# Two self-attentions of a decoder: scores with the keys as the stationary side, and a softmax over two halves of the keys

## What is computed

```python
# layer 0 (layer 1: same sizes, bias = -slope_h * sqrt(i - j) under the causal mask)
q = (x @ wq.T).reshape(B, N, 32, 128).transpose(0, 2, 1, 3)
k = (x @ wk.T).reshape(B, N, 8, 128).transpose(0, 2, 1, 3)      # 8 groups of 4 heads
v = (x @ wv.T).reshape(B, N, 8, 128).transpose(0, 2, 1, 3)
s = einsum('bhgnd,bhmd->bhgnm', q, k) * scale                    # 64 x 64 per batch and head
p = softmax(where(causal, s, -inf))
o = einsum('bhgnm,bhmd->bhgnd', p, v)
x = layernorm(x + o @ wo.T)
```

## Time and profile before

| | |
|---|---|
| median of 3 runs | 2332.91 us (2332.28 to 2333.55) |
| the profiled execution | 2332.89 us, its span 2331.0 us |
| PE busy | 2224.3 us, 95% of the span |
| DVE / ACT / POOL busy | 1300.0 / 781.4 / 772.1 us |
| first self-attention, second self-attention | about 0 to 563 us, about 1080 to 1680 us |
| DMA queue of SP | 22.4% of 16 engines' span |

### The profile page before, as it was taken

The page is one execution under the profiler, slowest core; times in us unless marked ns, Lnnn a source line. Parts: engine busy times, 40 slices in busy tenths (PEclk is TensorE's granted clock), DMA queues, the critical chain, the costliest instruction groups (busy, mean ns, idle before and its releaser), DMA issues.

```text
span 2331.0 us, 33907 instructions
## 1 busy us (share of the span) xinstructions
PE 2224.3 (95%) x11762; PEld 1769.8 (76%) x11762; DVE 1300.0 (56%) x2151; ACT 781.4 (34%) x1475; POOL 772.1 (33%) x709
## 2 busy tenths in 40 slices
PE   8999999997999989999899999999989999999978
PEld 6888888885555547887788888888878888887867
DVE  3454444447677733334345444444766767766766
ACT  2233222223677742222233232222333333232321
POOL 4222222202343336344422122221454344434233
PEclk9999999999999999999899999999999999999989
DMA  4212221221000032230222332222222222222120
GB/s 165 72 58 79 81 79 51 68 55 47 12 17 18 14 126 95 86 108 0 86 72 65 82 82 73 55 73 55 70 65 68 61 61 81 63 72 54 32 78 37
DMA packets 120545, 152.41 MB, mean 65 GB/s; under 512 B 16272, under 2 KB 67984, under 8 KB 119952
## 3 DMA queue, kind: packets, MB, share of 16 engines
q1 hardware_dynamic: 120464, 151.33, 22.4%
HBM read 124.02 MB, written 27.26 MB: 65 GB/s over the span
## 4 chain that ended last, share of the span: by engine, by line
PE 80%; issue 7%; DVE 7%; POOL 4%; ACT 2%; DMA 0%; POOLq 0%; DVEq 0%; ACTq 0%; SPq 0%
PE banks L283 20%; PE banks L285 19%; PE banks L284 18%; PE banks L598 7%; PE banks L641 3%; PE banks L1279 3%; PE banks L1263 2%; POOL f_wl L1690 1%; PE banks L1245 1%; PE banks L1252 1%; PE banks L1215 1%; PE banks L1231 1%; POOL f_il L1698 1%; DVE st L351 1%; PE banks L1269 1%
## 5 line engine op out<-in xcount | busy, mean ns | idle before, releaser
L283 PE MATMUL banks<-xTh,wh 128*128 128x512 f32 x1024 | 418.5, 409 | 11.7 <-DVE xTl L1965 7.5
L285 PE MATMUL banks<-xTh,wl 128*128 128x512 f32 x1024 | 404.3, 395 | 0.0
L284 PE MATMUL banks<-xTl,wh 128*128 128x512 f32 x1024 | 403.2, 394 | 0.0
L283 PE MATMUL banks<-woh,oth 128*128 128x512 f32 x768 | 313.5, 408 | 16.3 <-DVE X L936 7.0
L284 PE MATMUL banks<-wol,oth 128*128 128x512 f32 x768 | 301.8, 393 | 0.0
L285 PE MATMUL banks<-woh,otl 128*128 128x512 f32 x768 | 301.7, 393 | 0.0
L1031 POOL TENSOR_TENSOR sc_sb<-sc_sb,rs 128x512 f32<-128x512 f32 x96 | 103.7, 1083 | 553.2 <-DVE rs L890 553.2
L936 DVE TENSOR_TENSOR X<-banks,X 128x512 f32<-128x512 f32 x192 | 132.0, 688 | 272.9 <-PE banks L285 272.0
L733 ACT ACTIVATE q_sb<-banks 128x512 f32<-128x512 f32 x192 | 114.6, 597 | 402.0 <-PE banks L285 402.0
L283 PEld LDWEIGHTS banks<-xTh,wh 128*128 128x128 f32 x1024 | 195.2, 191 | 52.5 <-issue 9.3
L285 PEld LDWEIGHTS banks<-xTh,wl 128*128 128x128 f32 x1024 | 194.6, 190 | 43.6
(11 more groups left out here) (214 smaller groups left out, 4010.6 us busy)
## 6 DMA issues: line engine op xcount, KB each, us to landing
raw<-in_a_in SPq DMA_DIRECT2D x144, 256.0 KB, 2.8
raw<-in_a_out SPq DMA_DIRECT2D x96, 256.0 KB, 2.8
turned<-pq SPq DMA_DIRECT2D x384, 64.0 KB, 1.8
pt<-turned SPq DMA_DIRECT2D x96, 256.0 KB, 2.8
f_q<-in_f_q SPq DMA_DIRECT2D x21, 512.0 KB, 3.8
f_s<-in_f_s SPq DMA_DIRECT2D x21, 512.0 KB, 5.3
X<-in_x SPq DMA_DIRECT2D x1, 2048.0 KB, 10.7
x_craw<-in_ctx SPq DMA_DIRECT2D x8, 256.0 KB, 2.7
```

The lines of the kernel that those rows point to most:

```text
L283: nc.tensor.matmul(out, w_hi, x_hi, start=start, stop=False)
L284: nc.tensor.matmul(out, w_hi, x_lo, start=False, stop=False)
L285: return nc.tensor.matmul(out, w_lo, x_hi, start=False, stop=stop)
```

## The change

In `attn0` and `attn1`:

- The score product is turned: 64 columns of k are stationary and all 256 query columns move. Four calls a pair, 8 instructions; the calls with `b = 0` write partitions 0 to 63, those with `b = 1` partitions 64 to 127 of the same bank. A key now stands on each partition.
- DVE transposes 32x32 blocks straight from PSUM. A partition then holds a query and 32 of its 64 keys; the other 32 keys are 32 partitions away. DVE scales and adds the bias (now laid out for this, `bias_t`), and maximum, subtraction, exponential and sum go over each half apart.
- New event `SW`: PE multiplies the 32 columns of maxima and sums with a permutation matrix (`swap`), which brings each partition the numbers of the other half. New event `SX`: DVE copies them, subtracts the maxima, caps at 80; ACT takes the exponential; DVE multiplies, adds and takes the reciprocal. POOL normalises.
- A second DVE transposition of 32x32 blocks puts the keys back on the partitions, directly into `pt`. `turned` is no longer used there: 64 times five DMAs go. The bias of `attn1` comes in 8 DMAs a group, not 2.
- The list of events is new, and all engines follow it as it stands: `later` and `order` go. In the changed kernel the line numbers are higher.

The diff, cut to the parts that matter:

```diff
+        ev = events("U_0 VT1- SU3- PT0- SX2- U_1 SW3- TR2- SX3- WS0- WS1- U_2 PV0- PT1- TR3- WS2- WS3- U_3 WO0- PV1- U_4 PT2- "
+                    "WO1- U_5 PV2- WO2- SC0 SD0 EX0 PT3- WO3- SC1 SU0 SD1 EX1 U_6 PV3- SW0 WO4- SX0 SU1 U_7 SW1 TR0 WO5- SX1 "
+                    "U_8 TR1 WO6- U_9 WO7- SC2 SD2 EX2 U_10 SU2 SC3 SD3 EX3 U_11 SW2 VT0")
     if not project:
         if rms:
             return events("PT0- PV0- WO6-- SS3- PT1- WO7-- WS0- WS1- SC2- SD2- WS2- WS3- EX2- SU2- PV1- SC3- TR2- WO0- SD3- EX3- "
...
-            sq_turned = sb("sq_turned", [P, 32, 32])
+            sq_turned = shared[:, :].rearrange("p (n d) -> p n d", n=32)
+            bias_t = shared[:, 0:256]
...
-                        src = st.bias_in[i, r] if isinstance(i, int) else \
-                            st.bias_in[bass.ds(i, 1), r].rearrange("o p n -> p (o n)")
-                        sp.dma_start(bias[r, :, :], src.rearrange("p (c g s) -> p c g s", c=2, g=2)[:, :, h, :]
-                                     ).then_inc(ld_b, 16)
+                    for k in range(4):
+                        for h in range(2):
+                            r = slice(32 * h, 32 * h + 32)
+                            src = st.bias_in[i, r] if isinstance(i, int) else \
+                                st.bias_in[bass.ds(i, 1), r].rearrange("o p n -> p (o n)")
+                            sp.dma_start(bias_t[32 * k:32 * k + 32, :].rearrange("q (g h s) -> q g h s", g=G, h=2)[:, :, h, :],
+                                         src.rearrange("q (g s) -> q g s", g=G)[:, :, 32 * (k % 2):32 * (k % 2) + 32]
...
-                    if before and c in (1, 3) and not st.rms:
-                        move_out(i - 1, 2 + c // 2)
-                    if before and c in (2, 4) and not st.rms:
-                        move_in(i - 1, 1 + c // 2)
...
+                if not st.rms:
+                    for m in range(4):
+                        t, b = m // 2, m % 2
+                        col = pair * 2 * P + m * S
+                        last = nc.tensor.matmul(pb[2][64 * b:64 * b + 64, t * G * S:(t + 1) * G * S], k_sb[:, col:col + S],
+                                                q_sb[:, 4 * (pair % 2) + m, :], start=True, stop=True)
+                    last.then_inc(A["sc_done"], 1)
+                    return
                 for c in range(2):
                     for m in range(4):
                         col = pair * 2 * P + m * S
...
+            def swap_halves(i, pair):
+                st.need(pe, "s_sum", 4 * i + pair + 1)
+                st.need(pe, "s_link", 5 * (4 * i + pair) - 4)
+                if isinstance(i, int) and i == 0 and pair == 0:
+                    pe.wait_ge(A["swap_set"], 2)
+                nc.tensor.matmul(pb[4][:, 32 * pair:32 * pair + 32], swap[:, :], stat[:, pair, :], start=True,
+                                 stop=True).then_inc(A["s_swap"], 1)
 
             def square_sums(i, j):
...
                             r = slice(64 * b, 64 * b + 64)
-                            last = nc.tensor.matmul(PVB[b][:, cols], v_part[r, 2 * pair + t, :], by_query[p_part][r, t],
+                            p = by_query[p_part][r, t] if st.rms else (pth, ptl)[p_part][r, cols]
+                            last = nc.tensor.matmul(PVB[b][:, cols], v_part[r, 2 * pair + t, :], p,
                                                     start=v_part is vh and p_part == 0, stop=v_part is vl)
...
                         v_high(j, n)
-                    elif kind == ("EX" if st.rms else "SC"):
+                    elif kind == "EX":
                         exponentials(j, n)
+                    elif kind == "SX":
+                        st.need(act, "s_link", 5 * (4 * j + n) + 3)
+                        nc.scalar.activation(rel[:, n, :], rel[:, n, :], ACT.Exp).then_inc(A["s_rel"], 1)
                     elif kind == "PT":
-                        pt_wait(act, st, j, n, 1)
+                        if st.rms:
+                            pt_wait(act, st, j, n, 1)
+                        else:
+                            st.need(act, "t_done", 4 * j + n + 1)
...
-                        last = nc.vector.scalar_tensor_tensor(
-                            sc_sb[:, pair, 4 * c:4 * c + 4, :],
-                            pb[2][:, c * 4 * S:(c + 1) * 4 * S].rearrange("p (t s) -> p t s", t=4), st.scale, b[:, c],
-                            ALU.mult, ALU.add)
-                    last.then_inc(A["s_out"], 1)
+                    whole = rows.rearrange("p c s -> p (c s)")
+                    by_key = whole.rearrange("p (c k) -> p c k", k=32)
+                    nc.vector.transpose(whole, pb[2][:, :]).then_inc(A["s_turn"], 1)
+                    st.need(dve, "s_turn", 4 * i + pair + 1)
+                    if st.per_head_bias:
+                        two = whole.rearrange("p (t n) -> p t n", t=2)
+                        both = bias_t.rearrange("p (o n) -> p o n", o=1).to_broadcast([P, 2, G * S])
+                    else:
+                        two = rows
+                        both = bias_t[:, 0:S].rearrange("p (o n) -> p o n", o=1).to_broadcast([P, 8, S])
+                    nc.vector.scalar_tensor_tensor(two, two, st.scale, both, ALU.mult, ALU.add).then_inc(A["s_out"], 1)
                     st.need(dve, "s_out", 4 * i + pair + 1)
+                    nc.vector.tensor_reduce(stat[:, pair, 0:16], by_key, AX_X, ALU.max).then_inc(A["s_max"], 1)
+                    st.need(dve, "s_max", 4 * i + pair + 1)
+                    nc.vector.tensor_tensor(by_key, by_key, spread(stat[:, pair, 0:16]), ALU.subtract).then_inc(A["s_sub"], 1)
+                    return
                 nc.vector.tensor_reduce(smax[:, pair, :], rows, AX_X, ALU.max).then_inc(A["s_max"], 1)
                 st.need(dve, "s_max", 4 * i + pair + 1)
                 nc.vector.tensor_tensor(rows, rows, spread_rows(smax[:, pair, :]), ALU.subtract).then_inc(A["s_sub"], 1)
 
+            def spread(col):
+                return col.rearrange("p (c o) -> p c o", o=1).to_broadcast([P, 16, 32])
+
+            def relate_halves(i, pair):
+                link = 5 * (4 * i + pair)
+                st.need(dve, "s_swap", 4 * i + pair + 1)
+                nc.vector.tensor_copy(other[:, pair, :], pb[4][:, 32 * pair:32 * pair + 32]).then_inc(A["s_link"], 1)
+                st.need(dve, "s_link", link + 1)
+                nc.vector.tensor_tensor(rel[:, pair, :], other[:, pair, 0:16], stat[:, pair, 0:16],
+                                        ALU.subtract).then_inc(A["s_link"], 1)
+                st.need(dve, "s_link", link + 2)
+                nc.vector.tensor_scalar(rel[:, pair, :], rel[:, pair, :], 80.0, None, ALU.min).then_inc(A["s_link"], 1)
+                st.need(dve, "s_rel", 4 * i + pair + 1)
+                nc.vector.tensor_tensor(total[:, pair, :], other[:, pair, 16:32], rel[:, pair, :],
+                                        ALU.mult).then_inc(A["s_link"], 1)
+                st.need(dve, "s_link", link + 4)
+                nc.vector.tensor_tensor(total[:, pair, :], total[:, pair, :], stat[:, pair, 16:32],
+                                        ALU.add).then_inc(A["s_link"], 1)
+                st.need(dve, "s_link", link + 5)
+                nc.vector.reciprocal(inv[:, pair, :], total[:, pair, :]).then_inc(A["s_rec"], 1)
+
             def sums(i, pair):
                 st.need(dve, "exp_done", 4 * i + pair + 1)
+                if not st.rms:
+                    rows = sc_sb[:, pair, :, :].rearrange("p c s -> p (c s)").rearrange("p (c k) -> p c k", k=32)
...
 
                 st.need(dve, "p_ready", 4 * i + pair + 1)
+                if not st.rms:
+                    st.need(dve, "pt_ready", 4 * i + pair - 1)
+                    nc.vector.transpose(pt[:, pair % 2, :],
...
@@ -913,8 +992,10 @@
                         q_square_sums(j, n)
                     elif kind == "SS":
                         q_mean_square(j, n)
-                    elif kind == ("SD" if st.rms else "SC"):
...
             def normalise(i, pair):
                 st.need(pool, "s_rec", 4 * i + pair + 1)
                 rows = sc_sb[:, pair, :, :]
+                if not st.rms:
+                    rows = rows.rearrange("p c s -> p (c s)").rearrange("p (c k) -> p c k", k=32)
+                    nc.gpsimd.tensor_tensor(rows, rows, inv[:, pair, :].rearrange("p (c o) -> p c o", o=1).to_broadcast(
+                        [P, 16, 32]), ALU.mult).then_inc(A["p_ready"], 1)
+                    return
```

More of the change, by code:

```diff
@@ L439, in pt_wait @@
         def pt_wait(eng, st, i, pair, more):
-            wait(eng, pt_in[pair % 2], 16 * (16 * st.index + 2 * i + pair // 2 + more))
+            wait(eng, pt_in[pair % 2], 16 * (2 * i + pair // 2 + more))
         def late_bank(st, t):
@@ L518, in step @@
             def step(i, before, more):
-                first, second = (1, 2) if st.rms else (0, 1)
                 for c in range(5):
```

92 lines of the change are left out of this document (54 added, 38 removed).

## The result

The changed kernel takes 2380.05 us, median of 4 runs (2379.19 to 2383.95), the kernel before beside it 2333.23 (2332.28 to 2334.78). The ratio is 1.0203, 95% interval 1.0186 to 1.0221: 47 us slower, where +24 was forecast. The profiled execution of the changed kernel is the longest of its four, 2383.95 us with a span of 2382.0.

The account below looks back on a forecast made before the run. PE was taken to bound the kernel, busy 329.82 of 330 us. Its work -17, steady waits +32, first groups +3 and tails +6 made +24 us on 2332.91: 2357 us, range 2318 to 2388.

Parts of the forecast that it names:

- the term of the waits: PE's waits in steady groups of both self-attentions: 2.3 us in each of 7 groups of 2 stages, +32 us.
- the main case: Whole kernel: partial overlap in the score product plus new PE waits, 2357 us (2342 to 2370), chance 0.38.
- rival 2: Score product: no overlap between column halves, 2.0 us a product, +0.43 a pair, kernel 2389 us; chance 0.22.
- Scratch trips: Self-attentions: removing the trips gives 1.2 us at the most, counted as zero.
- Score product: PE, each pair: the turned product takes about 1.3 us instead of 1.79, -0.5, bounds +0.2 and -0.7.
- rival 3: Score product: column halves overlap fully, -0.47 a pair with the swap product, kernel 2347 us; chance 0.13.
- Swap product: PE, each pair: the added 128x32 product costs 0.23 us in full, 64 times.
- Swap of pair 1: PE in each steady group waits 1.2 us for DVE's sum of pair 1.
- First output tile: Steady groups: low parts 0.9 us late, last weight parts 0.4 more; not all new, so PE waits +0.8 us.
- The 0.3 at the swap of pair 3: Steady groups: PE waits 0.3 us there for the first small copy of pair 2.
- first groups and tails: Start and end of both self-attention stages: new PE waits of +3 us in first groups, +6 in tails.
- Rival 1: Self-attentions: all steady waits go, leaving -17 and +3 us for tails and first groups, 2319 us; chance 0.25.

Follow-up runs that it names:

- Experiment 10: Kernel before the change, with only the scratch trips of both self-attentions left out: 2331.32 us, ratio 0.9999.
- experiment 9: Changed kernel, with all four calls of a pair's score product on the same column half from group 1 on: 2421.48 us.
- experiment 2: Changed kernel, with DVE taking the sum of pair 1 ahead of the six small operations of pair 0: 2376.46 us.
- Experiment 1: Changed kernel, with SP loading the last weight chunk ahead of the eight bias DMAs in the second self-attention: 2370.72 us.
- Experiment 5: Changed kernel, with the first two low parts of the output weights ahead of the relation of pair 3: 2373.31 us.
- Experiment 4: Changed kernel, with the second transpositions of pairs 2 and 3 moved behind the weight splits: 2362.51 us.
- experiment 7: Changed kernel, with weight chunk ahead of bias, sum of pair 1 ahead of pair 0's relation, and a new order at the group seam: 2312.83 us.

## Why the prediction was right in direction and half in size

Slower was forecast with 0.68, and the time lies in the range, but the term of the waits was sized at half. That the range held is in part luck: the main case was given as 2342 to 2370, and 2380 lies outside it. The range reached to 2388 for the sake of rival 2, whose mechanism, no overlap in the score product, did not come.

- **Scratch trips, counted zero: right.** Experiment 10 measures -0.0001 of the time, with 0.1% to either side.
- **Score product, -0.5 a pair: right to 0.08 us, by the wrong picture.** Forecast were 5 steps of 0.224 us, each call's second instruction over the next call's first. The calls of the two halves run side by side throughout, -0.58. This is rival 3's overlap, which the Trainium skill (TensorE: Matmul & The Clock Gate, part 3) speaks for: different column groups run concurrently. The trace agrees, 1.21 us on two halves against 2.07 on one. Rival 3's price for it, -0.47 with the swap, was too good: entry and exit cost 0.3 us here (1.21 less 4 x 0.224), where I took 0.2. Rival 2 (no overlap) is what experiment 9 built by hand; its 2.0 us a product was right. (Its sum takes +7 "as above", where above stand 3 + 6; with 9 it gives 2391.)
- **Swap product, +0.23: right,** 0.24. With the score product it makes -22 us, forecast -17.
- **Swap of pair 1, 1.2 us a group: right.** The trace shows 0.8 to 0.9, which by the reckoning below cost 1.0 to 1.2. The small operations of `SX` follow each other at 0.21, not 0.28, so that the chain was shorter by some tenths than laid out; experiment 2 removes the wait entirely.
- **First output tile, +0.8: the step that failed.** PE now waits there 0.81 and 1.37 us in the first self-attention, and 2.42 and 1.34 in the second, which cost 2.7 and 4.3 us a group. The text allowed for POOL's normalisation and for two weight parts 0.4 us late. Three things were not in it or were counted too small. (a) "SP ... gets 6 more bias DMAs a group in the second stage; nobody waits for them within 30 us": nobody waits for the bias, but the last weight chunk stands behind those DMAs and their wait on SP's queue, and POOL splits it ahead of its normalisation. Experiment 1: 9 us. (b) The normalisation now coincides with DVE's low parts of the weights. Each was costed at its length alone; together they take 0.85 and 0.4 us more. The next two low parts beside POOL's split take 2.29 us, 0.5 more than before the change. Experiment 5: 7 us in the median, not clear of the noise. (c) The transposition at the head of DVE's queue, named but only as part of 0.9 us. Experiment 4: 17.5 us. The three overlap, and their shares in the 65 us of waits are not separated.
- **A wait as the trace shows it is less than what it costs.** The 0.81 us at 277.84 stand between a matmul at 276.64 and one at 278.18: 1.54 us, where two spacings make 0.46. The wait costs 1.08, 0.27 more than shown, since the start is measured against a modelled end and the matmul behind it is spaced 0.34. With three waits a group that is 0.8 us, and 0.81 + 1.37 + 0.76 (5.3 in 7 times, swap of pair 1) + 0.8 gives 3.7 of the 3.8 us a group of the first self-attention. The 0.3 at the swap of pair 3 is not among the waits: L960 is listed once a group.
- **Sum.** -22 from PE's work, +27 (7 x 3.8) and +38 (7 x 5.5) from steady waits, together +43. The two profiled executions differ by 51 us, the medians by 47, so first groups and tails have 8 or 4 left, where +9 was forecast. The sum of +24 had +32 where +65 belongs.
- **Rival 1 (PE stays covered, 2319 us)** was wrong for this order of events and right for another: experiment 7 gave 2313. The rival had 0.25, and what spoke for it, that DVE is idle half of the time, is what experiment 7 uses.

## What to carry to other kernels

A queue is costed by what stands behind an added instruction, not by who reads its result: nobody needed the bias soon, but the load behind its DMAs and their wait cost 9 us. When a chain gets longer, the first thing to try is the order of events at the seam of the loop; here, with the one load moved, it was worth 67 us (2380 to 2313), three times the 22 us that the change saves on PE. Where a move puts a DVE instruction with two inputs in SBUF beside a POOL one that reads SBUF, one or both last longer than in the rows where each was alone.

## What the runs showed of the hardware

- Plain float32 products with 64 stationary columns run two at a time when they write different halves of the partitions, in both orders of the calls that were tried: 1.21 us for 8 of 256 moving columns, 2.07 on one half.
- DVE's two-input instruction of 128x512 in SBUF takes 0.68 us alone and, where it begins within a POOL instruction that reads SBUF, nearly always 0.95 to 1.78 in these traces (1.54 in the case shown). With one input in PSUM it keeps 0.68 to 0.69 there.
- Two gains on PE's path can add to more than their sum: 9.3 and 3.6 us alone, 24.8 together, because a wait of 2.4 us in each group let the clock fall behind it in one order (0.97 over 440 us) and hardly in the other (0.99), and was under 1 us when both were applied (1.00).
